# Second attention of a four-stage block: the output bias leaves TensorE and is added to the residual by GpSimd

## The reference

```
x = x + tanh(g_xattn[0]) * L0_xattn(ctx, layernorm(x))
x = x + tanh(g_ffn[0])   * L0_ffn(layernorm(x))            # mixture of experts
x = x + tanh(g_xattn[1]) * L1_xattn(layernorm(x), ctx)     # the stage changed here
x = x + tanh(g_ffn[1])   * L1_ffn(layernorm(x))
```

```
q = x @ Wq.T;  k = ctx @ Wk.T;  v = ctx @ Wv.T
y = softmax(mask(q k^T / 4)) v
return y @ Wo.T + bo
```

## Time and profile before

| | |
|---|---|
| median of three runs | 3353.44 us |
| the profiled execution | 3354.25 us |
| its span, first to last instruction | 3352.5 us |
| busy over the span: TensorE, VectorE, ScalarE, GpSimd | 93%, 73%, 49%, 23% |
| this stage, from its first load to its last addition | about 2653 to 3121.5 us of the span |

### The profile page before, as it was taken

One profiled execution on the slowest core, in us unless ns is written; L12 is line 12 of the kernel. 1 busy time (PEld: TensorE's weight loads), 2 busy tenths in 40 slices (PEclk: granted clock), 3 DMA queues, 4 the chain that ended last, 5 costly groups with the idle time before them and its releaser, 6 DMA issues. The chain is left out here.

```text
span 3352.5 us, 63415 instructions
## 1 busy us (share of the span) xinstructions
PE 3113.9 (93%) x20868; PEld 2885.6 (86%) x20868; DVE 2460.4 (73%) x4826; ACT 1645.7 (49%) x3104; POOL 764.2 (23%) x1372
## 2 busy tenths in 40 slices
PE   4999999999999999999699999999999879999588
PEld 3999999999999999999577788998989778888476
DVE  5777777777777777777766777777778756666787
ACT  2555555555555555555333322222222256666587
POOL 2222222223222222221111111111111123332220
PEclk9999999999999999999799999999999889999799
DMA  3000000000000000000200222423333200000000
GB/s 93 16 14 11 12 15 11 11 14 12 13 14 13 12 9 14 14 6 3 57 5 5 72 89 82 118 92 112 93 87 93 68 1 1 0 0 0 26 20 32
DMA packets 117456, 113.94 MB, mean 34 GB/s; under 512 B 39823, under 2 KB 83144, under 8 KB 117192
## 3 DMA queue, kind: packets, MB, share of 16 engines
q1 hardware_dynamic: 117192, 110.62, 11.4%
HBM read 105.33 MB, written 5.24 MB: 33 GB/s over the span
## 5 line engine op out<-in xcount | busy, mean ns | idle before, releaser
L437 ACT ACTIVATE x_pth<-x_ps 128x512 fp32r<-128x512 f32 (+1 forms) x768 | 376.4, 528 | 252.4 <-PE x_ps L671 249.7
L956 ACT ACTIVATE moe_sil<-moe_ps,moe_b 128x512 f32<-128x512 f32 x256 | 176.4, 689 | 561.1 <-PE moe_ps L1110 552.1
L539 DVE TENSOR_TENSOR x_ptl<-x_ps,x_pth 128x512 fp32r<-128x512 f32 (+1 forms) x768 | 402.9, 552 | 32.6 <-ACT x_pth L437 20.5
L457 ACT ACTIVATE x_p<-x_p,x_nmx 128x1178 f32<-128x1178 f32 x256 | 327.6, 1280 | 131.6 <-DVE x_p L563 131.3
L1133 PE MATMUL moe_ps<-moe_w2z,moe_gh 128*128 128x256 f32 (+1 forms) x1280 | 370.0, 289 | 1.8 <-DVE moe_gl L1073 1.8
L563 DVE TENSOR_SCALAR_CACHE_REDUCE x_p<-x_ps 128x1182 f32<-128x1182 f32 x256 | 354.5, 1385 | 22.4 <-PE x_ps L682 13.0
L671 PE MATMUL x_ps<-ident,x_p 128*128 128x128 f32 x2560 | 365.7, 274 | 2.1 <-DVE x_ptl L539 1.8
L1133 PE MATMUL moe_ps<-moe_w2z,moe_gl 128*128 128x256 f32 x1280 | 362.0, 283 | 0.0
L1133 PE MATMUL moe_ps<-moe_w2l,moe_gh 128*128 128x256 f32 x1280 | 361.9, 283 | 0.0
L697 PE MATMUL x_ps<-x_pth,x_vh 128*128 128x256 f32 x1152 | 346.3, 301 | 0.0
L697 PE MATMUL x_ps<-x_ptl,x_vh 128*128 128x256 f32 x1152 | 325.3, 282 | 0.0
(11 more groups left out here) (375 smaller groups left out, 8149.2 us busy)
## 6 DMA issues: line engine op xcount, KB each, us to landing
moe_gate<-moe_cw_rows SPq DMA_DIRECT2D x512, 128.0 KB, 2.9
xres<-in_x_dram SPq DMA_DIRECT2D x4, 1024.0 KB, 9.3
x_rawv<-in_L_xattn_Wkv_dram SPq DMA_DIRECT2D x16, 256.0 KB, 2.9
x_rawk<-in_L_xattn_Wkv_dram SPq DMA_DIRECT2D x32, 128.0 KB, 2.1
x_rawq<-in_L_xattn_Wq_dram SPq DMA_DIRECT2D x32, 128.0 KB, 2.2
x_rawo<-in_L_xattn_Wo_dram SPq DMA_DIRECT2D x32, 128.0 KB, 2.0
moe_w1r<-in_L_ffn_w_dram SPq DMA_DIRECT2D x8, 512.0 KB, 5.8
moe_w2r<-in_L_ffn_w_dram SPq DMA_DIRECT2D x4, 1024.0 KB, 10.1
```

The lines of the kernel that those rows point to most:

```text
L437: act.activation(turn_dst(pth, x, lo, hi), turn_src(x, g), ACT.Copy).then_inc(hi_done, 1)
L457: act.activation(p[:, w % 4, DUP:DUP + R_KV], p[:, w % 4, DUP:DUP + R_KV], ACT.Exp, bias=nmx[:, w % 2:w % 2 + 1], scale=-1.0, accum_out=su ...
L539: last = dve.tensor_tensor(turn_dst(ptl, x, lo, mid), turn_src(x, g)[:, 0:mid - lo, :], turn_dst(pth, x, lo, mid).bitcast(F32), ALU.subtract)
L956: act.activation(dst[:, q % 2, :], ps[:, HID + q % 2, :], ACT.Silu, bias=bias).then_inc(silu_done, 1)
```

## The change

The bias row is now loaded into all 128 partitions (`tbo`, 128 KB instead of 1 KB) and multiplied once by g on VectorE. In each step with w%4 == 3, GpSimd adds it to the two tiles of `xres` that belong to chunk `CPB*b + w//4`. It first waits for the layernorm that has read these tiles (`y_ready`). VectorE's addition of the projected chunk waits for that (`bo_added`). `project` keeps its 12 full products and loses the four single-row ones. The tanh of the gate now signals on `rooted`, which so counts to two.

```diff
-        bor = sb("bor", [1, DIM])
-        boh, bol, one1 = sb("boh", [1, DIM], F32R), sb("bol", [1, DIM], F32R), sb("one1", [1, P], F32R)
+        tbo = sb("tbo", [P, DIM])
...
-            sp.dma_start(bor[:, :], A["L1_xattn_bo"].rearrange("(a d) -> a d", a=1)).then_inc(d_in, 16)
+            sp.dma_start(tbo[:, :], A["L1_xattn_bo"].partition_broadcast(P)).then_inc(d_in, 16)
...
-            pool.tensor_copy(one1[:, :], ones[0:1, :]).then_inc(set_up, 1)
             own.wait()
+            pool.memset(ones[0:1, 0:1], 1.0).then_inc(set_up, 1)
...
                 if w < STEPS:
                     keep_tail(b, w)
+                if w % 4 == 3 and w < STEPS:
+                    C = CPB * b + w // 4
+                    part = xres[:, bass.ds(2 * C, 2), :]
+                    pool.wait_ge(y_ready, C + 1)
+                    pool.sem_inc(alone_pool, 1)
+                    pool.tensor_tensor(part, part, tbo[:, :].unsqueeze(1).broadcast_to([P, 2, DIM]), ALU.add).then_inc(bo_added, 1)
...
                 spread_v(0, g)
+            pool.wait_ge(ready, 1)
             steps(pool, step)
...
-            act.activation(tg[:, :], tg[:, :], ACT.Tanh).then_inc(tanhed, 1)
+            act.activation(tg[:, :], tg[:, :], ACT.Tanh).then_inc(rooted, 1)
...
                     dve.wait_ge(d_in, 16 * ND)
-                    own.link(dve.tensor_copy(boh[:, :], bor[:, :]))
-                    dve.tensor_tensor(bol[:, :], bor[:, :], boh[:, :].bitcast(F32), ALU.subtract).then_inc(ready, 1)
+                    dve.wait_ge(rooted, 1)
+                    dve.tensor_scalar(tbo[:, :], tbo[:, :], tg[:, 0:1], None, ALU.mult).then_inc(ready, 1)
+            dve.wait_ge(rooted, 2)
+            newton_rsqrt(own, dve, var[:, :], root[:, :], rstd[:, :])
             dve.wait_ge(rooted, 1)
-            newton_rsqrt(own, dve, var[:, :], root[:, :], rstd[:, :])
-            dve.wait_ge(tanhed, 1)
...
                     dve.wait_ge(wo_done, S + 1 + WO0)
+                    dve.wait_ge(bo_added, S + 1)
...
-            pe.wait_ge(ready, 1)
...
                     out = ps[:, WO, t * DIM:(t + 1) * DIM]
-                    pe.matmul(out, one1[:, :], boh[:, :], start=True, stop=False)
-                    pe.matmul(out, one1[:, :], bol[:, :], start=False, stop=False)
                     for k in range(KT):
                         for i, (o, w) in enumerate(((oh, wh), (oh, wl), (ol, wh))):
-                            last = pe.matmul(out, o[:, c % 2, k, t * P:(t + 1) * P], w[3][:, k, :], start=False, stop=(k == 1 and i == 2))
+                            last = pe.matmul(out, o[:, c % 2, k, t * P:(t + 1) * P], w[3][:, k, :], start=(k == 0 and i == 0), stop=(k == 1 and i == 2))
```

More of the change, by code:

```diff
@@ L1263, in ctx_attention_stage @@
         pre_done, pre_hi, pre_lo = sem("pre_done"), sem("pre_hi"), sem("pre_lo")
-        tanhed, stats, rooted, ready = sem("tanhed"), sem("stats"), sem("rooted"), sem("ready")
+        stats, rooted, ready = sem("stats"), sem("rooted"), sem("ready")
         y_ready, x_turned, x_hi, x_lo = sem("y_ready"), sem("x_turned"), sem("x_hi"), sem("x_lo")
@@ L1271, in ctx_attention_stage @@
         wo_done, x_added, tails_set, alone_pool = sem("wo_done"), sem("x_added"), sem("tails_set"), sem("alone_pool")
-        tail_kept = sem("tail_kept")
+        tail_kept, bo_added = sem("tail_kept"), sem("bo_added")
         block = ctx.enter_context(nc.Block())
```

## The result

| | before | after |
|---|---|---|
| median of five runs each | 3355.18 us | 3336.50 us |
| lowest and highest | 3353.08, 3362.2 | 3335.26, 3340.85 |
| the profiled execution's span | 3352.5 us | 3334.8 us |

The ratio is 0.9942, with a 95% interval of 0.9928 to 0.9957: between 14 and 24 us less. The predicted time was 3336.4 us. A second set of five runs gave 3337.83 us, ratio 0.9950 (0.9936 to 0.9964). So the time was met. That it was met to 0.1 us is luck: the five runs after spread over 5.6 us, and the median before rose from 3353.44 with three runs to 3355.18 with five. The question is whether the terms were met.

What follows compares the result with a forecast made beforehand. TensorE was taken to bound the stage, with each projection on the path for its full length. The terms 14.4 + 1.5 + 1.6 - 0.5 = 17.0 us, taken from 3353.4, gave 3336.4 us, range 3332.5 to 3343.

Steps and rivals of the forecast that it cites:

- The single-row products: TensorE's projections: without four single-row products each takes 1.52 us instead of 2.55; 14 chunks gain 1.03 each, 14.4 us.
- The fifteenth projection: In the drain, beside ScalarE's last read and VectorE's reciprocal, for which GpSimd's last scaling waits: gain 0.
- The clock: TensorE's clock fell twice in the 220 us looked at; both falls go, 2 x 0.8 = 1.6 us gained.
- The last projection: Alone on the path at the stage's end, 4.11 us before: gains between 1.1 and 2.3, taken as 1.5 us.
- The load: Start of the stage: the bias load grows from 1 to 128 KB and delays TensorE, 0.5 us lost.
- The additions: GpSimd's 16 additions of 128x512, 21 us of work, are hidden: 0, or 3.9 us if batch ends show them.
- the argument with 1.14 us of room: At batch ends GpSimd idles only 1.14 us before the scaling, which comes 0.15 us late, perhaps 0.3.
- Falls that stay: Rival 1: TensorE's clock falls stay or come elsewhere; gain 15.4 us, time 3338.0, with two more 3339.6; chance 0.28.
- Partial takeover: Rival 2: another engine or wait takes over in part; gain about 9.8 us, time 3343.6; chance 0.16.
- GpSimd's addition against VectorE: Rival 3: additions hold the shared SBUF port and VectorE stands still, up to 21 us, time 3357; chance 0.04.
- The dearer load: Rival 4: the bias load costs 1.2 us or more instead of 0.5, time 3337.1; within the forecast's 0.50.

Runs made afterwards that it cites:

- before_again: The kernel before the change, profiled once more without an edit: 3352.81 us.
- bias_last: The changed kernel with the bias load behind the gate's and its own semaphore value, so TensorE doesn't wait for it: 3338.77 us, 0.9953 of the kernel before.
- no_add: The changed kernel without GpSimd's 16 additions and the wait for them, the bias left out of the output: 3338.24 us, 0.9946 of the kernel before.
- vector_add: The changed kernel with the bias addition on VectorE instead of GpSimd, at the same w: 3337.82 us, 0.9944 of the kernel before.
- longer_add: The changed kernel with one further GpSimd operation of 128x1024 behind each bias addition: 3339.15 us, 0.9947 of the kernel before.
- long_add: The changed kernel with three further GpSimd additions of 128x1024 behind each bias addition: 3358.56 us, 1.0012 of the kernel before.
- spread_later: The changed kernel with GpSimd's first spreading of keys and values waiting for VectorE's first layernorm of the stage: 3333.39 us, 0.9928 of the kernel before.

## Why the prediction was right

**The single-row products, 14.4 us: right, and 0.5 too small.** The forecast had 1.03 for 14 chunks. Thirteen projections became 1.05 us shorter. From the first to the 13th that is 12 of them, 12.6 us (306.59 in `before_again`, without a fall, less 293.95). The 13th and the 14th gave 2.29, that is 1.05 and 1.24; for the fourteenth the forecast missed that without idle time ahead of it one change between the kinds more falls into the stream. Together 14.9. The source of the price, the length of the query's products, was right to 0.01 us (1.52, measured 1.51). The fifteenth projection is hidden as said: its gain stands as idle time ahead of the last, 3.74 instead of 2.50 us.

**The clock, 1.6 us: right here, but of two falls whose number is luck.** Both went: 308.24 - 306.59 = 1.65 us. `before_again` had one fall, of 1.24 us (47.94 instead of 46.70 us from the 13th projection to the last), so the same comparison could have given 1.2. That the falls belong to the single-row products was argued from the rows and is supported by counts: 10 falls in three profiles with them, none in nine without. The stretch of 220 us at clock 1.00 that the forecast put beside the two falls begins behind them; it doesn't hold them.

**The last projection, 1.5 us: mis-sized, 1.99.** I took it near the slow end of 1.8 to 3.0 us, because the clock would fall. In the profile it fell only during the last products (0.12 us apart up to 3102.0, then about 0.2), so it took 2.12. Over the other profiles with these 12 products it takes 1.96 to 2.97 us, so the bounds were right, and where between them an execution falls is luck too.

**The load, -0.5 us:** measured -0.40, but within scatter, as `bias_last` shows.

**The additions, 0: right, with a wrong margin.** `no_add` shows the 0, `vector_add` that the engine doesn't matter. But the argument with 1.14 us of room counted the wrong thing; `longer_add` and `long_add` put the true room at a batch end between 3.3 and 7.5 us. The other half of the argument, that what stands behind the addition is wanted later, is what held, and the first to be late is the tail, which the forecast had as wanted one step on.

**What the forecast didn't have:** the earlier stages ended 1.03 us later, and the stretch to the first projection was 0.58 shorter. No edit touches the first. The second varies from 97.1 to 100.3 us over the profiles that do the same there, so both are taken as scatter between executions. With them 14.93 + 1.65 + 1.99 - 0.40 + 0.58 - 1.03 = 17.7, the span's. The forecast's four terms so gave 18.2 us where it had 17.0, and what it didn't have took 0.45 off. The difference of the medians is 18.7; the time was met as closely as it was because the median before, which it was counted from, had meanwhile risen by 1.7. By its own terms the lower end of the stated range is 3332.6 (3336.4 - 0.8 - 3), not 3332.5; nothing hangs on it.

**The rivals.** Falls that stay: not seen between the first and the 14th projection. Partial takeover: ruled out by the 2.43 us of VectorE's idling and by `no_add`. GpSimd's addition against VectorE: reciprocals of 128x256 stayed at 1.74 to 1.75 us and layernorms at a median of 410 ns, so it costs nothing here; the mechanism exists, as `spread_later` shows, where other operations meet. The dearer load: open; the means differ by 0.4 us within a scatter of 1.1.

## What to carry to other kernels

Read the price of a product from distances between starts, and compare with a stretch of the same engine that lacks the suspect: here the query's products gave 1.03 of a true 1.05 us. Where single-row products stand in a stream of full ones, the products were the smaller part of their price here (0.47 us) and the changes between the kinds the larger (0.59). Padding them to full rows saved the larger part; grouping them should save some of it, which no run tested. Better, give a sum like this to an engine with idle time. How late an engine may be is not the idle time ahead of its instruction but the time until somebody waits for the result: follow that consumer in the timeline, or lengthen the work and see.

## What the runs showed of the hardware

- A change between products of one row and of 128 costs 0.19 us each time, beside 0.12 us for a product of 256 columns with either number of rows. Three changes and four products make 1.05 us, four and four 1.24. Padding to 128 rows took 0.59 us off each chunk.
- The clock fell in the steady part only where single-row products stood in the projection, and more often with more of them (2, 1, then 7), with the same 0.9 us of idling ahead. It also fell once in `long_add`, without them, at the end of a wait of 2.84 us, but not at three waits of 2.83 to 2.86 us before it, and in every profile around the last projection, ahead of which TensorE idles 2.0 us or more.
- Beside GpSimd's spreading VectorE's products of 128x32 took 1.13 us instead of 0.19 and the two parts of the layernorm 2.46 instead of 0.74, but the reciprocal of 128x256 its usual 1.74. One wait on GpSimd took 3.4 us off the stretch to the first projection.
